# The SiLU gates of the first stage on ScalarE's Silu, in place, at the end of a block's preparation

## The reference

```python
# graph part: x += (where(adj < 1, exp(-(1/adj - 1)^2 / 0.5), 0)) @ (layernorm(x) @ W + B)
# Mamba-2 part, on h = layernorm(x):
zxbcdt = h @ W_in                                  # 256 -> z 512, xBC 640, dt 8
conv = conv_b + sum(xp[:, k:k + L, :] * conv_w[:, k] for k in range(4))
xBC = silu(conv)
xh, Bmat, Cmat = split(xBC)                        # 512, 64, 64
...                                                # chunked state space sums over 128 tokens here
Y = Y_diag + Y_off + xh * D
Y = Y * silu(z)
Y = Y * rsqrt(mean(Y * Y) + EPS) * norm_w
x = x + (Y @ W_out) @ W_lin + b_lin
```

## Time and profile before

| | |
|---|---|
| median of 3 executions | 2474.83 us (2473.66 to 2478.3) |
| the profiled execution | 2480.63 us, span of its instructions 2478.7 us |
| first stage | about 0 to 1106 us |
| busy over the span: PE | 2237.4 us (90%) |
| VectorE | 1918.4 us (77%) |
| ScalarE | 1565.3 us (63%) |
| GpSimd | 1137.2 us (46%) |
| granted TensorE clock, mean | 0.957 of full speed |

### The profile page before, as it was taken

One profiled execution on the slowest core, in us unless ns is written; L12 is line 12 of the kernel. 1 busy time (PEld: TensorE's weight loads), 2 busy tenths in 40 slices (PEclk: granted clock), 3 DMA queues, 4 the chain that ended last, 5 costly groups with the idle time before them and its releaser, 6 DMA issues.

```text
span 2478.7 us, 26139 instructions
## 1 busy us (share of the span) xinstructions
PE 2237.4 (90%) x8852; PEld 1398.2 (56%) x8852; DVE 1918.4 (77%) x2207; ACT 1565.3 (63%) x2448; POOL 1137.2 (46%) x914
## 2 busy tenths in 40 slices
PE   7998999999999999988999999999999997765998
PEld 4444545454544545545766676666666663433886
DVE  5676877777877776423999899999999998996765
ACT  4677777777777765424575756666675756663444
POOL 2101212222121213201987888888887887891000
PEclk9998999999999999999999999999999998687999
DMA  5233232323233323233323232332333220113121
GB/s 206 94 110 106 86 120 93 119 77 119 77 119 95 112 92 111 92 98 103 111 93 120 94 109 88 108 113 86 119 103 102 94 89 23 47 48 110 35 77 43
DMA packets 116310, 238.06 MB, mean 96 GB/s; under 512 B 8226, under 2 KB 65954, under 8 KB 115794
## 3 DMA queue, kind: packets, MB, share of 16 engines
q1 hardware_dynamic: 107106, 204.00, 25.4%
q0 software_dynamic: 8528, 31.36, 3.6%
q10 hardware_dynamic: 544, 1.05, 0.1%
HBM read 216.06 MB, written 20.32 MB: 95 GB/s over the span
## 4 chain that ended last, share of the span: by engine, by line
PE 39%; DVE 23%; ACT 14%; issue 13%; POOL 12%; DMA 0%; DVEq 0%; ACTq 0%; SPq 0%; POOLq 0%
PE ps L633 9%; POOL dB L2249 8%; DVE h L1430 6%; DVE wgt L1105 4%; ACT wgt L1617 3%; PE ps L675 3%; ACT E L1617 3%; DVE acc L1402 2%; PE ps L797 2%; PE ps L919 2%; ACT ps L1617 2%; ACT th L1617 2%; POOL acc L2232 2%; DVE wgt L1098 2%; POOL du L2245 2%
## 5 line engine op out<-in xcount | busy, mean ns | idle before, releaser
L2249 POOL TENSOR_TENSOR dB<-du,bc 128x512 f32<-128x512 f32 x512 | 656.0, 1299 | 91.0 <-DVE h L1430 87.6
L1430 DVE TENSOR_TENSOR_SCAN h<-ps,hst,dB 128x512 f32<-128x512 f32 x512 | 643.5, 1272 | 46.4 <-ACT ps L1617 35.4
L1617 ACT ACTIVATE ps<-dt,cols 128x512 f32<-128x512 f32 x512 | 351.4, 687 | 271.1 <-DVE h L1430 269.2
L633 PE MATMUL ps<-wgt,msg 128*128 128x512 f32 x1024 | 499.5, 601 | 16.3 <-DVE wgt L1105 14.8
L675 PE MATMUL ps<-raw,msg 128*128 128x256 f32 x1792 | 451.5, 388 | 0.9 <-ACT hb L1617 0.9
L919 PE MATMUL ps<-consts,h 128*128 128x128 f32 x2048 | 338.5, 293 | 98.9 <-DVE acc L1402 53.2
L919 PEld LDWEIGHTS ps<-consts,h 128*128 128x128 f32 x2048 | 258.5, 150 | 271.9 <-DVE acc L1402 110.8
L675 PEld LDWEIGHTS ps<-raw,msg 128*128 128x128 f32 x1792 | 331.1, 196 | 73.9 <-issue 39.3
L633 PEld LDWEIGHTS ps<-wgt,msg 128*128 128x128 f32 x1024 | 188.0, 192 | 222.6 <-issue 193.8
L1617 ACT ACTIVATE wgt<-wgt 128x1024 f32<-128x1024 f32 x256 | 258.2, 1047 | 66.9 <-DVE wgt L1098 65.3
L2232 POOL TENSOR_TENSOR acc<-acc,part 128x512 f32<-128x512 f32 x160 | 210.1, 1313 | 80.8 <-ACT part L1617 77.1
(11 more groups left out here) (324 smaller groups left out, 3534.5 us busy)
## 6 DMA issues: line engine op xcount, KB each, us to landing
raw<-in_adjT SPq DMA_DIRECT2D x256, 512.0 KB, 3.7
bc<-tmp_bc SPq DMA_DIRECT2D x64, 512.0 KB, 4.8
E<-tmp_bc POOLq DMA_DIRECT2D x32, 512.0 KB, 4.3
xb<-in_xT POOLq DMA_DIRECT2D x8, 512.0 KB, 4.7
tmp_x<-xb POOLq DMA_DIRECT2D x8, 512.0 KB, 3.1
x<-tmp_x SPq DMA_DIRECT2D x8, 512.0 KB, 5.0
tmp_x<-x SPq DMA_DIRECT2D x8, 512.0 KB, 3.7
raw<-tmp_xn SPq DMA_DIRECT2D x8, 512.0 KB, 4.1
```

The source lines that it names most:

```text
L633: x = e.matmul(P[d][:, :], msg[:, j, d * 128:(d + 1) * 128], wgt[g % NW][:, l, :], start=j == 0, stop=j == NJ - 1)
L1430: e.tensor_tensor_scan(hr[n % 3][:, m, :], PS[4 + k % 2].t[:, :], dBr[k % 4][:, :], hst[:, n % 16, m:m + 1], ALU.mult, ALU.add).then_inc(S ...
L1617: return e.activation(out, in_, func, bias=bias, scale=scale)
L2249: e.tensor_tensor(dBr[k % 4][:, :], du[:, m, :], bcr[i % 3][:, n % 2, :], ALU.mult).then_inc(S("dB"), 1)
```

## The change

The tanh and the products go. At the end of `pre_a`, when the last tap is done, ScalarE does Silu in place: on `cc` in two instructions of 128x1024, on the two halves of the fifth tile, which it writes to their places, and on z in two of 128x1024. Each raises `sil` by one, six a block as before, but in another order: PE's `inner` waits for four (all of `cc`) and VectorE's L1239 for six. The halving shrinks to the second stage's columns, and the scaling of `Win` goes; so do ScalarE's wait for `sil` ahead of the norm and two waits for `setup`. The generators keep their number of steps, with empty ones in place of the gates. Numbers of the lists: the product's last step in `order_first` at 0.92 of the way, not 1; two more product steps ahead of step 4 of `ssd`; the last weight at 0.90, not 0.95; the steps of `pre` start 0.01 earlier.

```diff
-HALVED = COLS["D0"][0]
+HALVED = slice(COLS["cw1"][0], COLS["D0"][0])
...
-        order_first = braid(("pre", NPA, 0, 1), ("p", NP, 0, 1))
+        order_first = braid(("pre", NPA, 0, 1), ("p", NP, 0, 0.92))
...
-        FILLS, SEND, WFIRST, WLAST, EVAC, PREND = ((7, 2), (38, 1), (50, 2), (55, 1), (58, 2)), 58, 0, 0.95, 0.995, 0.95
+        FILLS, SEND, WFIRST, WLAST, EVAC, PREND = ((4, 2), (7, 2), (38, 1), (50, 2), (55, 1), (58, 2)), 58, 0, 0.90, 0.995, 0.95
...
-                at += [(x, "pre") for x in spread(NPA, 0, PREND)]
+                at += [(x, "pre") for x in spread(NPA, -0.01, PREND)]
...
# tensor, inner
-                    w.wait_ge(S("sil"), 6 * ib + 6)
+                    w.wait_ge(S("sil"), 6 * ib + 4)
...
# vector, pre_a
                     if m % 2:
-                        for i, what in enumerate((cc[:, m - 1:m + 1, :], z[:, m - 1:m + 1, :])):
-                            yield
-                            w.wait_ge(S("tanh"), 5 * ib + m + i)
-                            e.scalar_tensor_tensor(what, (th, sq)[i][:, :, :], 1.0, what, ALU.add, ALU.mult).then_inc(S("sil"), 1)
-                            yield
-
-                yield
-                w.wait_ge(S("tanh"), 5 * ib + 5)
-                for i in range(2):
-                    e.scalar_tensor_tensor(cc[0:64, 4 + i, :], th[64 * i:64 * i + 64, 0, :], 1.0, cc[64 * i:64 * i + 64, 4, :], ALU.add,
-                                           ALU.mult).then_inc(S("sil"), 1)
+                        yield from [None] * 4
+                yield
                 yield
...
# vector, outer
-                    w.wait_ge(S("sil"), 6 * ib + 4)
+                    w.wait_ge(S("sil"), 6 * ib + 6)
...
-                    w.wait_ge(S("d_Win"), 16)
-                    e.tensor_scalar(Win[:, :, 0:512], Win[:, :, 0:512], 0.5, None, ALU.mult).then_inc(S("setup"), 1)
...
# scalar, pre_a
-                w.wait_ge(S("sil"), 6 * ib)
...
                     if m % 2:
-                        w.wait_ge(S("conv"), 20 * ib + 4 * m + 4)
-                        w.wait_ge(z_use(ib, m).evac, z_use(ib, m).n)
-                        for i, what in enumerate((cc[:, m - 1:m + 1, :], z[:, m - 1:m + 1, :])):
-                            w.wait_ge(S("sil"), 6 * ib + m + i - 2)
-                            act((th, sq)[i][:, :, :], what, ACT.Tanh).then_inc(S("tanh"), 1)
-                            yield from (None, None)
+                        yield from [None] * 4
+
                 w.wait_ge(S("conv"), 20 * ib + 20)
-                w.wait_ge(S("sil"), 6 * ib + 3)
-                act(th[:, 0, :], cc[:, 4, :], ACT.Tanh).then_inc(S("tanh"), 1)
+                for k in range(0, 4, 2):
+                    act(cc[:, k:k + 2, :], cc[:, k:k + 2, :], ACT.Silu).then_inc(S("sil"), 1)
+                for i in range(2):
+                    act(cc[0:64, 4 + i, :], cc[64 * i:64 * i + 64, 4, :], ACT.Silu).then_inc(S("sil"), 1)
+                for k in range(0, 4, 2):
+                    w.wait_ge(z_use(ib, k + 1).evac, z_use(ib, k + 1).n)
+                    act(z[:, k:k + 2, :], z[:, k:k + 2, :], ACT.Silu).then_inc(S("sil"), 1)
                 yield from (None, None)
```

More of the change, by code:

```diff
@@ L688, in pre_a @@
                 w.wait_ge(v.evac, v.n)
-                w.wait_ge(S("setup"), 7)
+                w.wait_ge(S("d_Win"), 16)
                 w.wait_ge(b.evac, b.n - 1)
@@ L761, in outer @@
                     yield
-                    w.wait_ge(S("setup"), 7)
+                    w.wait_ge(S("setup"), 6)
                     w.wait_ge(Y.evac, Y.n - 1)
@@ L1067, in _ @@
             w.wait_ge(S("d_consts"), 32)
-            e.tensor_scalar(cols[:, 0:HALVED], cols[:, 0:HALVED], 0.5, None, ALU.mult).then_inc(S("setup"), 1)
+            e.tensor_scalar(cols[:, HALVED], cols[:, HALVED], 0.5, None, ALU.mult).then_inc(S("setup"), 1)
             w.wait_ge(S("setup"), 1)
```

## The result

| | before | after |
|---|---|---|
| median of the runs on the same chip (range), us | 2474.24 (2473.46 to 2478.3) | 2454.27 (2450.24 to 2455.81) |
| time of the profiled execution, us | 2480.63 | 2455.74 |
| its span, us | 2478.7 | 2453.8 |
| mean period of a block in the five turns between like blocks (starts of L809), us | 119.49 | 117.86 |

The ratio is 0.9913, with a 95% interval of 0.9896 to 0.9931: 20 us faster by the medians, 24.9 by the two profiled executions; the interval leaves 1 out, so the change is real, and it is under 1%. The forecast was 2457 us, a sum of -18.1 from profile to profile, with faster at 0.79.

A forecast was written before the change was run, and what follows sets the result against it. PE bounds the first stage, except at block turns, where a chain through all engines decides. Terms -6.5 - 5.0 - 6.6 = -18.1 us take 2480.63 to 2462.5, less 5.8 for the profiled run's distance from the median: 2457 us, range 2438 to 2476.

The forecast's parts named there:

- The forecast case: Whole kernel: 2457 us, its own range 2442 to 2472, chance 0.62.
- first turn and its block: First turn: earlier convolution end brings L693 2.1 us forward, plus 0.86 and 2.05: -5.0 us.
- last two blocks: Last two blocks: hs wait -2.9, slow-clock pieces -1.3, three loads -3.8, against a burst delay of 2.2: -6.6 us.
- What is removed: First stage: 56.4 us of VectorE gates and 32 ScalarE table loads (41 us) go; nothing comes back directly.
- The turn of the block: Block turn: the Silu burst makes L693 1.6 us later, less 0.86 for one pair: a loss of about 0.75 us.
- the extra pair: Ahead of L693: one more product matmul pair than before (11 for 10), worth 0.86 us.
- the same two collisions: L1105 at the turn: GpSimd's L2143 and L2138 still overlap it by 1.45 and 1.05 us, 2.50 together.
- The rest of the block: Mid-block: PE's gaps at L755 (1.37 us) and L788 (0.68) close, a gain of 2.05 us.
- in this count already: Block turn: the pair before has its second exponential ahead of the table load, saving 2 us, already counted.
- A: Rival: the turn closes, half its 4.62 us of waits and the 1.2 GHz stretch go: 2428 us, chance 0.13.
- C: Rival: slower, as L586, the pair and L693 wait in turn for late ScalarE: 2485 us, chance 0.12.
- B: Rival: nothing to be told, gains at L755 and L788 fail or collisions get worse: 2470 to 2475 us, chance 0.13.

The follow-up runs named there:

- e1: The changed kernel with the three order numbers put back, so only the gates are changed: 2486.54 us, ratio to before 1.0036.
- e11: e4 with GpSimd's product of E for each block's first chunk moved behind VectorE's L1153, in six blocks: 2429.52 us, ratio to before 0.9808.
- e9: The changed kernel without the early fill at step 4, weights kept at 0.90: 2475.66 us, ratio to before 0.9989.
- e12: The changed kernel with the last weights back at 0.95, early fill kept: 2479.85 us, ratio to before 1.0009.
- e3: The changed kernel with an unused ScalarE copy of 128x1024 (1.06 us) added behind the Silus: 2465.85 us, ratio to before 0.9956.
- e10: The changed kernel leaving out seven of eight heads in GpSimd's two first-chunk products, from the second block on: 2440.95 us, ratio to before 0.9856.
- e13: e11 without the early fill: 2441.62 us, ratio to before 0.9855.
- e8: The changed kernel with each pair of Silus set where the tanh stood, spread over the block: 2472.85 us, ratio to before 0.9986.
- e4: The changed kernel with z's two Silus moved ahead of the wait for the convolution's last tap: 2441.77 us, ratio to before 0.9861.

## Why the prediction came out right

The forecast case held: time, range, and sign. That the time came within 3 us is in part luck. From profile to profile the gain was 6.8 us larger than the sum; the prediction took off 5.8 us for the distance of the profiled execution from the median, and after that distance was only 1.5. The terms, against the profiles (difference of the starts of L809):

| stretch | predicted | measured |
|---|---|---|
| first turn and its block | -5.0 | -8.6 |
| five turns and their blocks | -6.5 | -8.2 |
| last two blocks | -6.6 | -8.2 |
| sum | -18.1 | -25.0 |

**What is removed** was right: 62 table loads, and no direct return from VectorE's 56 us. e1 shows it at its barest, with all those gates gone and the kernel slower.

**The turn of the block.** The Ln stands 9.09 us after the load (561.50, 570.59) where the prediction had 8.9, and 8.16 separate Ln and second exponential (8.18 forecast). L693 comes 24.4 us after the load in the longer kind of block, for 24.3 forecast, and 25.3 in the shorter kind. The 1 us more is the clock: the half-clock piece stood behind L693 before and now falls ahead of it in this turn, on the matmuls of L633. The loss in the turn beside the extra pair was 1.75 (23.47 - 20.86 - 0.86) or 0.87 for 0.75. "L586 and L633 waiting 2 to 3 us each" is what came (2.05, 2.23), in all but one of the five turns; in that one L633 waits 0.54, since PE already runs slowly ahead of it. So the longer kind of block, 118.41 us, is the block of the prediction: 1.1 us won for 1.3. The shorter kind wins 2.0 by where its half-clock piece falls, and no term of the sum has that: it is luck, and 2.7 us of the 8.2.

**The port clash.** The assumption that the same two collisions stand was right (4.90 us for 4.91). By the Trainium skill (SBUF — State Buffer, the section on the two separate sides) an operation of VectorE with two inputs in SBUF and one of GpSimd that reads SBUF exclude one another for whole instructions; the traces agree in the sizes, 2.36 us for the pair without GpSimd (e11) and 4.90 with. Its lock for whoever starts first does not tell who comes next: in after GpSimd's xdec got in before the second L1105 was through, as in the earlier trace rows.

**The rest of the block.** Both gaps closed: 2.06 us of idle time to 0.06, against 2.05 forecast. The exact term of the sum.

**The orders.** Here the prediction was right in its sum and wrong in its reasons. It priced what the orders put ahead of L693 at "0.86", one product pair. The profile of e9 has 5.0 us a period for the absence of the early fill (two pairs): the idle time grows by them and the half-clock piece behind it triples. And it treated the place of the last weights as 2 us "in this count already"; the profile of e12 has 5.0 a period for it as well (122.84), because L1131 stands in the queue behind that pair. Both profiles lie some 6 us above the medians, which give 21 and 26 us in all. Had I been asked for the gates alone, I would have been wrong in the sign, as the expectation of e1 shows: 2458 to 2463 for 2486.54.

**First turn.** The step that failed is the place of the last tap: the load starts at 208.25, not 210.6, and L693 comes 4.2 us earlier for 2.1. Behind it the block is 4.4 shorter for 2.9: the mid-block gap of 2.05, the pair, and about 1.6 of clock (98.21 us of PE work before for 95.77 with two instructions fewer).

**The last two blocks.** The wait of 4.10 for hs fell to 0.22, by 3.9 for 2.9 forecast. I counted "2.6 us" of half-clock pieces and half of it as won. In the last block but one PE's busy time fell from 82.27 to 76.59 with the clock at 1.00 all through: 5.7 us, four times my term. The loads priced at 3.8 would show in three waits: L788's fell from 1.91 to nothing and, in the last block, to 1.48, L809's from 1.25 to 0.47, 3.1 in all. The last block took back 4.6 for the 2.2 less 0.8 and a load that I gave it: L733 waits 2.03 for the copies of messages, L755 3.08 for hs (2.43 before), and a half-clock piece of 7 us follows where there was none. Windows of after for both:

```profile
929.76:995.33 65.57, 64.19 (x259) 36.62 (x259) 38.19 (x55) 23.76 (x56) 18.22 (x18) 1.00 0.22 74
995.33:1068.70 73.37, 66.22 (x256) 37.85 (x256) 22.15 (x38) 29.20 (x66) 19.35 (x15) 0.95 0.27 86
```

**The rivals.** A did not come by itself, but e11 is A nearly to the letter (half of the turn's idle time gone, 2.56 of 4.62 left, and no piece at half clock: 2429.52 for 2428), with what A lacked: a shorter burst and no clash. C was real in mechanism: more idle time, and a longer stretch at 1.2 GHz behind it. e9 has that, with 10 us in the place of 3.5. What kept the change out of C was its orders: without the early fill it is level with before (2475.66), with late weights 2479.85, and with the old orders 2486.54, C's 2485, though there by a wait for L1131 that C does not have. B did not come.

## What to carry to other kernels

When a change gathers work on an engine into one burst, first look at what is half made when the burst begins: anything whose second half stands behind the burst will hold its consumer's in-order queue, and everything behind it, for the burst's whole length. Price idle time of TensorE with the half-clock piece that may follow it, and hold idle times against each other only where the clock is the same; a filler of two product pairs in the waits was worth 5 us a block in one kernel here and 1.7 in another. And test the two halves of a change apart before believing either: here each alone lost and both together won.

## What the runs showed of the hardware that I had not expected

- The granted clock falls in pieces, and a piece that lies where PE waits is free: turns of equal length have 5.54 us of idle time at full clock and 3.86 with a piece in after (22.58 and 22.59 us), 6.63 and 4.95 in e3 (23.68 and 23.67), 4.59 and 2.94 in e10 (21.64 both).
- Behind the turn a piece followed in before (4.62 us idle in the turn at full clock) and in e13 (3.96), one of 10 us in e9 (7.26), and none in e11 (2.56) or e10 (4.59). The total does not decide it, and neither does the order of the instructions: e8 has turns of 20.85 us with 4.0 idle and the same waits, of which three are followed by a piece and one is not. The Trainium skill (TensorE: Matmul & The Clock Gate, on what is actually happening) lets the gate follow how busy the array has been of late, and these runs agree as far as they go; the exact rule they don't show.
- The same order of instructions settled into two kinds of block that alternate (117.5 and 118.4 us), from the clock alone.
- A table load cost no more than its own 1.28 us: 561.50 to 562.79, and 553.93 to 555.23 in e4; of the 62 in after all but one are followed by the next instruction 1.29 us after their start. Silu in place took 1.05 us for 128x1024, as in the second stage, and 0.62 for 64x512 (mean of 16).
